# Writing out a loop over pairs of images on all five engines

## The reference

```
x = x + relu(batchnorm(conv3x3(sign(layernorm_over_channels(x)), sign(w) * alpha) + b))
t = tokens of x (3136 per image, 128 features each)
n = layernorm(t)
w = n @ wr + br                      # a router weight for each token
chosen = the 1567 tokens of an image with the largest w
t = t + n + where(chosen, w * (gelu(n @ w1 + b1) @ w2 + b2), 0)
```

## Time and profile before

| | us |
|---|---|
| median of 3 runs (lowest, highest) | 2188.62 (2183.65, 2190.84) |
| the profiled execution: its time | 2182.01 |
| its span, first to last instruction | 2180.2 |
| mean granted clock | 0.981 |
| PE, DVE, ACT, POOL busy | 92%, 77%, 56%, 43% |

### The profile page before, as it was taken

One profiled execution on the slowest core, in us unless ns is written; L12 is line 12 of the kernel. 1 busy time (PEld: TensorE's weight loads), 2 busy tenths in 40 slices (PEclk: granted clock), 3 DMA queues, 4 the chain that ended last, 5 costly groups with the idle time before them and its releaser, 6 DMA issues. The chain is left out here.

```text
span 2180.2 us, 37651 instructions
## 1 busy us (share of the span) xinstructions
PE 2012.3 (92%) x9515; PEld 1019.5 (47%) x9515; DVE 1677.1 (77%) x4759; ACT 1210.3 (56%) x2030; POOL 939.7 (43%) x714
## 2 busy tenths in 40 slices
PE   6999999995899999999999998999999999999995
PEld 3555555552344444444444444444444444444442
DVE  6777777775688878787888787788878787888875
ACT  3444444442656656556666565656666555666553
POOL 1000000003455556555655565555655555655543
PEclk9999999997999999999999999999999999999998
DMA  4344444442123333333333333332333332333313
GB/s 159 135 175 160 150 177 148 161 175 92 50 109 127 117 109 125 116 114 109 129 111 122 112 113 110 115 133 109 111 126 119 110 130 109 123 111 121 109 65 123
DMA packets 68758, 268.17 MB, mean 123 GB/s; under 512 B 22352, under 2 KB 27184, under 8 KB 64688
## 3 DMA queue, kind: packets, MB, share of 16 engines
q1 hardware_dynamic: 55264, 214.90, 27.1%
q10 hardware_dynamic: 13392, 52.29, 6.5%
HBM read 188.08 MB, written 77.87 MB: 122 GB/s over the span
## 5 line engine op out<-in xcount | busy, mean ns | idle before, releaser
L954 PE MATMUL ps<-hs,w_c 128*128 128x448 f32 x1792 | 771.7, 558 | 0.6 <-ACT yo L510 0.6
L500 ACT ACTIVATE hs<-ps,b1c,undo 128x448 f32<-128x448 f32 x896 | 609.3, 718 | 128.6 <-PE ps L945 120.8
L870 PE MATMUL ps<-yo,cwT 128*128 128x448 bf16 x2016 | 425.7, 356 | 0.0
L954 PEld LDWEIGHTS ps<-hs,w_c 128*128 128x128 f32 x1792 | 316.3, 192 | 210.2 <-issue 176.8
L417 POOL TENSOR_TENSOR tl<-tr,th 128x448 f16<-128x448 f32 x224 | 246.7, 1102 | 353.1 <-ACT th L535 240.9
L412 POOL TENSOR_TENSOR xb<-xb,zr 128x448 f32<-128x448 f32 x224 | 261.9, 1172 | 263.2 <-ACT zr L528 262.4
L943 PE MATMUL ps<-th,w_h 128*128 128x448 f16 x896 | 318.7, 356 | 17.7 <-ACT hs L500 17.5
L945 PE MATMUL ps<-th,w_l 128*128 128x448 f16 x896 | 316.4, 353 | 0.0
L944 PE MATMUL ps<-tl,w_h 128*128 128x448 f16 x896 | 316.3, 353 | 0.0
L424 POOL TENSOR_TENSOR yo<-yo,base 128x448 f32<-128x448 f32 x224 | 281.2, 1262 | 75.0 <-DVE yo L797 75.0
L510 ACT ACTIVATE yo<-ps,cols 128x448 f32<-128x448 f32 x224 | 141.5, 632 | 273.5 <-PE ps L954 272.7
(11 more groups left out here) (125 smaller groups left out, 2380.1 us busy)
## 6 DMA issues: line engine op xcount, KB each, us to landing
xb<-x SPq DMA_DIRECT2D x31, 1568.0 KB, 7.6
xb<-x SPq DMA_DIRECT2D x33, 896.0 KB, 4.7
gate_all<-gate_row ACTq DMA_DIRECT2D x32, 896.0 KB, 4.5
result<-yo SPq DMA_DIRECT2D x32, 896.0 KB, 3.5
y_int<-y SPq DMA_DIRECT2D x32, 784.0 KB, 3.7
xb<-x SPq DMA_DIRECT2D x33, 672.0 KB, 4.4
gate_all<-gate_row ACTq DMA_DIRECT2D x32, 672.0 KB, 5.6
result<-yo SPq DMA_DIRECT2D x32, 672.0 KB, 3.0
```

Source lines behind the costliest of these rows:

```text
L500: nc.scalar.activation(hs[(b + slot) % 2][:, j, :], ps[:, H_BANK + j, 0:T], ACT.Gelu_apprx_tanh, bias=b1c[:, j:j + 1], scale=undo[:, 1:2]) ...
L870: last = M(bank, cwT[:, t, :], sg[b][:, c * ROWS + dy:c * ROWS + dy + ROWS, dx:dx + SIDE], start=t == 0, stop=t == TAPS - 1)
L954: last = M(bank, w2_c[:, j, :], hs[(b + c) % 2][:, j, :], start=first, stop=final)
```

## The change

The five calls of `pairs` for the second phase become plain Python loops over the same range of n, so that `phase2` is emitted for each image with n as a number. `P2` goes. The first phase keeps its loops.

```diff
@@ -307,7 +307,6 @@
         P1 = (1, n_img - 1)
-        P2 = (3, n_img - 3)
@@ SyncE
-            pairs(sp, phase2, *P2, -2, n_img + 1)
+            for n in range(-2, n_img + 1):
+                phase2(n, n % 2)
@@ GpSimd
-            pairs(pool, phase2, *P2, -2, n_img + 1)
+            for n in range(-2, n_img + 1):
+                phase2(n, n % 2)
@@ ScalarE
-            pairs(act, phase2, *P2, -2, n_img + 1)
+            for n in range(-2, n_img + 1):
+                phase2(n, n % 2)
@@ VectorE
-            pairs(dve, phase2, *P2, -1, n_img + 1)
+            for n in range(-1, n_img + 1):
+                phase2(n, n % 2)
@@ TensorE
-            pairs(pe, phase2, *P2, -1, n_img + 1)
+            for n in range(-1, n_img + 1):
+                phase2(n, n % 2)
```

## The result

The changed kernel takes 2162.52 us (median of 4 runs, 2162.15 to 2164.79) beside 2189.73 for the kernel before on the same chip (2183.65 to 2193.62, now with a fourth run). The ratio is 0.9894, 95% interval 0.9869 to 0.992: faster by 1%, clear of noise. That is 23 us by the ratio, about 27 in the medians, where 41 were forecast (2147, range to 2160). The profiled executions give 2182.0 before and 2162.5 after, spans 2180.2 and 2160.5, so 19.7 us; the profiled execution of before (2182.0) is faster than all its timed runs, so differences between two traces come out smaller here than those between medians.

What follows compares the result with a forecast made beforehand. The prediction took TensorE (92% busy) as the busiest engine, with DVE waiting for code behind each taken branch of the loop. Savings of 34.3 + 5.9 + 0.4 = 40.6 us from 2188.6 gave 2147 us, range 2137 to 2160.

Steps and rivals of the forecast that it cites:

- Point 2: Register work on SyncE's queue delays the load of y's second part; 13 second images gain 0.45 us each, 5.9 us.
- Point 4: Register work on the other queues is read ahead while engines compute: nothing gained; 9 us if it isn't hidden.
- Point 1: DVE's stall behind the loop's 12 taken branches, and the clock's fall after some of them, go: 34.3 us saved.
- point 3: The odd image of the loop's first turn, 50.2 us against 49.55 written out: 0.4 us saved.
- Point 5: Code that PE and others now fetch in every pair costs nothing; delayed data packets would give back 13 us.
- A: Rival, 14%: only the stall goes, second images stay at 48.9 us, odd ones fall to 50.2; time 2159 to 2162.
- B: Rival, 15%: every pair runs like the written-out ones, 97.4 to 97.5 us, no slow clock; 47 to 48 us saved.
- C: Rival, 5%: no change; the loop costs the branch's own time, or DVE's stall is hidden; 2184 to 2193 us.
- D: Rival, 4%: slower; running straight on, DVE stalls at block ends too; with two stalls a pair 2218 us.

Runs made afterwards that it cites:

- x2: The kernel before with only VectorE's (DVE's) loop written out, the other four engines looped: ratio 0.9784 to the kernel before.
- x3: The changed kernel with VectorE's (DVE's) loop kept, all other engines written out: ratio 1.0043 to the kernel before.
- x6: The kernel before with VectorE's (DVE's) loop over four images a turn, 5 taken branches in place of 12: ratio 0.9875 to the kernel before.
- x11: The kernel before with VectorE (DVE) and SyncE written out, the other three engines looped: ratio 0.9737 to the kernel before.
- x12: The changed kernel with mean over deviation computed on GpSimd instead of VectorE and SyncE's loop kept: ratio 0.9814 to the kernel before.
- x7: The changed kernel with ScalarE's loop kept, all other engines written out: ratio 0.9737 to the kernel before.
- x14: The changed kernel with a useless 192-column ScalarE copy per image ahead of the 16-bit copy of the last chunk: ratio 0.9693 to the kernel before.
- x4: The changed kernel with mean over deviation computed on GpSimd instead of VectorE (DVE): ratio 0.9736 to the kernel before.
- x1: The changed kernel with GpSimd's loop kept, all other engines written out: median 2160.75 us, ratio 0.9856 to the kernel before.

## Why the prediction was wrong

The direction and the main mechanism (DVE's stall behind the taken branch) were right; the step that failed is the pair of points 2 and 4, that the second image of a turn gets 0.45 us shorter and that register work on the other queues is worth "nothing". The even images got 1.0 us longer instead, since one DVE instruction went from 1.01 to 3.09 us.

**Point 1 (34.3 us) with point 3 (0.4): right in mechanism, near in size by luck.** The odd images went from 628.9 + 50.2 = 679.1 us to 646.2, so 32.9 against 34.7. No issue wait and no slow clock is left. x2, x3 and x6 show that DVE's branch is the cause. The size is luck, as the part on the model images shows. The prediction also says that the 108 ns which the Trainium skill ("Advanced Engine Details and Errata", section Control Flow Timing) has for a compare-and-branch agree with the branch's own duration. DVE's is 63 ns: the two are alike only in being small beside 2.84 us.

**Points 2 and 4: −5.9 us forecast, +13.4 measured.** The even images went from 635.0 to 648.4 us. With the 1.8 us of point 1 these 19.3 are the 21.1 us between the 40.6 forecast and the 1314.1 − 1294.6 = 19.5 found. Point 2's mechanism is real: y's second part is issued 0.9 us behind wk, as forecast, here in SyncE's timeline of image 7 of the changed kernel, and x11 and x12 put its worth at 10 to 17 us over all 26 images, roughly, or 0.4 to 0.65 us each where 0.45 was taken.

```profile
930.33 0.48 SPq L383 DMA_DIRECT2D wk<-w_row  x1
...
931.27 0.43 SPq L334 DMA_DIRECT2D y<-y_int  x1
```

But the whole chain in front of it came later: counted from the image's first matmul (899.7) the issue is at 31.6, and not at 30.5. DVE's 3.09 us hold PE at L922, and rows, router and search follow. Point 4 looked at register work only as time on a queue that is or isn't hidden. ScalarE's is hidden, and still its copy comes 0.16 us earlier than before and 0.25 us earlier than in x7, where its loop is kept. With GpSimd's later start this changed how long another engine's instruction takes.

**Why the model images hid it.** I took 49.5 and 49.6 (images 1 and 29) for the odd images and 48.0 for the even ones. The busy time of L688 in windows of the kernel before, for image 1, image 2, images 3 to 28, and image 29, shows what these were:

```profile
602.60:652.10 49.50, 3.09 (x1) 1.00 0.30 107
652.10:700.10 48.00, 1.01 (x1) 1.00 0.34 123
700.10:2014.20 1314.10, 26.30 (x26) 0.99 0.32 117
2014.20:2063.80 49.60, 3.09 (x1) 1.00 0.33 120
```

The two images at 49.5 had the slow instruction in them and the one at 48.0 hadn't, and I had put the 1.5 us between them down to odd and even. x11 has the same: its images 1 and 29, slow, average 50.05 us, the 27 between them 48.4. (It isn't all: image 3 took 50.2 before without the slow instruction.) The loop's 26 images had it nowhere. In the changed kernel 25 of 26 have it, and most images came out like images 1 and 29. Point 1 fitted because its model carried the same loss that the changed odd images were to have. Without it all are as image 2 or a little over: x14 has 1253.0 / 26 = 48.19. The change could thus have saved 48.5 us (x4) to 61 us (x14) of the stretch, and gives back 29.0 to 41.6 of it at one instruction.

**Point 5: right.** In images 5 to 28 queue 8 has 44 code packets where there were none, queue 14 has 52 instead of 60, and no engine shows a new issue wait. That queue 8 is PE's follows from the experiments: x1, x3, x7 and x12 each keep one other engine's loop and have the 44 as well, and x2, x6 and x11, with PE looped, have none.

**The rivals.** A's time, 2159 to 2162, is nearest to the result, but not its reasons: its odd images were to be at 50.2 and its even ones at 48.9, they are at 49.7 and 49.9. B's 47 us is x2's gain by the ratio, but its reason, that every pair runs at 97.4 to 97.5, is not what x2 has (1279.6 / 13 = 98.4); x11 (96.8) and x14 (96.4) go below it. C and D are out: the branch costs 2.9 to 3.9 us, and running on costs no stall. D's bound was also worked out wrong: at 2.7 us a stall, 3.1 us a pair are eaten by 1.15 stalls and not one and a half. The condition that I named for the failure of the forecast as a whole, pairs over 99 us though the stalls are gone, is what the windows show (1294.6 / 13 = 99.6).

**What stays open.** Whether the last step from x11 (0.9737) to x14 (0.9693) is real, since the intervals overlap. Which of ScalarE's register instructions held its copy back in the loop; x7 shows only that its loop does. What starts GpSimd's first low part 0.27 us later in the changed kernel: writing out DVE and SyncE doesn't (x11 has 19.36), x1 and x7 show that GpSimd's and ScalarE's loops can stay for it, and PE's program, which is left, was not tried alone. And why the instruction waits through three of GpSimd's above a margin of 0.26 us.

## What to carry to other kernels

When one kernel contains the same body both looped and written out, compare them instruction by instruction (minimum, median and maximum of each line), and not only by the length of the stretch: a maximum of 3089 ns over a median of 1011 was in the trace before the change, and it was most of the error here. Hidden work isn't free to remove: it sets at which moment the instructions of two engines meet, here DVE's and GpSimd's. And write out the engines one at a time, the one that idles behind its branch first; DVE and SyncE alone gave 0.9737 where all five gave 0.9894.

## What the hardware did that I had not expected

- A small DVE instruction that meets GpSimd's stream waits for one GpSimd instruction (1.01 us) or for three in a row (3.09 us). It was three whenever the next GpSimd instruction's input had been ready 0.26 us or more before the present one ended, and one at 0.24 us or less (330 images in the traces of ten kernels).
- A useless ScalarE instruction of 0.36 us an image made the changed kernel 2% faster (0.9894 to 0.9693 of the time before).
- DVE's stall behind a taken branch is the same with two images in a turn and with four (2.9 us of idle time at most in both), ends 1.9 to 2.0 us behind the start of a code packet, and costs the kernel 2.9 us each by the traces and 3.9 by the ratio.
